# A third score buffer and two more projection buffers in a ViT tower's head loop, with the class key's columns copied by GpSimd one head later

## The reference

```python
def _layernorm(x, axis=-1, eps=1e-05): ...
for i in range(L):                                   # 4 layers
    qkv = h @ W_qkv[i]
    q, k, val = ...                                  # 16 heads of 64
    kr = (r @ W_r[i]).reshape(s_len, H, DH)
    AC = jnp.einsum('bqhd,bkhd->bhqk', q + u, k)
    BD = jnp.einsum('bqhd,khd->bhqk', q + v, kr)
    prob = jax.nn.softmax((AC + BD) * inv_sqrt_d, axis=-1)
    vec = jnp.einsum('bhqk,bkhd->bqhd', prob, val).reshape(b, s_len, H * DH)
    h = layer_norm(h + vec @ W_o[i], ln1_g[i], ln1_b[i])
    ff = jax.nn.relu(h @ W_ff1[i] + b_ff1[i]) @ W_ff2[i] + b_ff2[i]
    h = layer_norm(ff, ln2_g[i], ln2_b[i])
```

## Time and profile before

| | |
|---|---|
| median of three runs | 2712.31 us |
| the profiled execution | 2716.57 us |
| its span | 2714.8 us |
| granted TensorE clock, mean | 0.96 |
| TensorE busy | 2218.4 us, 82% |
| VectorE busy | 1825.3 us, 67% |
| ScalarE busy | 1611.2 us, 59% |
| GpSimd busy | 1180.7 us, 43% |

### The profile page before, as it was taken

One profiled execution on the slowest core, in us unless ns is written; L12 is line 12 of the kernel. 1 busy time (PEld: TensorE's weight loads), 2 busy tenths in 40 slices (PEclk: granted clock), 3 DMA queues, 4 the chain that ended last, 5 costly groups with the idle time before them and its releaser, 6 DMA issues. The chain is left out here.

```text
span 2714.8 us, 61320 instructions
## 1 busy us (share of the span) xinstructions
PE 2218.4 (82%) x19212; PEld 1637.8 (60%) x19213; DVE 1825.3 (67%) x5486; ACT 1611.2 (59%) x5053; POOL 1180.7 (43%) x2186
## 2 busy tenths in 40 slices
PE   0169989899988989889889889898898898733995
PEld 0146666666666666666666666676666666521663
DVE  8747777777767777777777777776777777643333
ACT  2136666666666667666666666666666666611221
POOL 3025445554555555544555555445645555102002
PEclk9679999999999999999999999999999999966998
DMA  5444333345553333454543333455433333074002
GB/s 168 95 109 104 92 92 92 92 107 138 137 141 93 92 92 92 108 135 114 148 105 89 94 92 92 126 128 152 105 91 93 92 93 92 18 190 140 29 27 78
DMA packets 386301, 282.99 MB, mean 104 GB/s; under 512 B 44859, under 2 KB 360371, under 8 KB 385355
## 3 DMA queue, kind: packets, MB, share of 16 engines
q1 hardware_dynamic: 379531, 262.37, 37.5%
q10 hardware_dynamic: 4864, 12.68, 1.3%
q0 software_dynamic: 1600, 4.23, 0.5%
HBM read 120.30 MB, written 57.82 MB: 66 GB/s over the span
## 5 line engine op out<-in xcount | busy, mean ns | idle before, releaser
L1248 ACT ACTIVATE E<-E,nb 128x257 f32<-128x257 f32 x1024 | 513.5, 510 | 38.3 <-DVE nb L1424 38.1
L969 PE MATMUL bk<-hin,w_sb 128*128 128x257 f16 x3072 | 424.7, 275 | 18.4 <-ACT rel L1186 9.0
L1424 DVE CUSTOM_DVE_ANT_0 E<-bk,cb 128x257 f32<-128x257 f32 x1024 | 390.1, 419 | 66.7 <-PE bk L1062 65.1
L1386 DVE TENSOR_TENSOR pt<-bk,pt 128x512 f16<-128x512 f32 x512 | 354.3, 692 | 63.7 <-ACT pt L1235 53.9
L1017 PE MATMUL bk<-ident,E 128*128 128x128 f32 x2048 | 323.2, 280 | 84.6 <-ACT E L1248 61.3
L969 PEld LDWEIGHTS bk<-hin,w_sb 128*128 128x128 f16 x3072 | 296.3, 98 | 72.5 <-issue 14.1
L1017 PEld LDWEIGHTS bk<-ident,E 128*128 128x128 f32 x2048 | 221.8, 141 | 164.1 <-ACT E L1248 150.5
L1235 ACT ACTIVATE pt<-bk 128x512 f16<-128x512 f32 x512 | 306.9, 599 | 6.5 <-PE bk L1017 6.5
L917 POOL TENSOR_SCALAR wf<-wf 128x256 f32<-128x256 f32 x216 | 92.8, 429 | 432.6 <-DMA wf<-in_w_dram 260.9
L1061 PE MATMUL bk<-kh,qs 128*128 128x257 f16 x1024 | 254.9, 275 | 9.7 <-DMA kl<-rk 9.5
L1062 PE MATMUL bk<-kl,qs 128*128 128x257 f16 x1024 | 254.5, 275 | 0.0
(11 more groups left out here) (275 smaller groups left out, 4406.3 us busy)
## 6 DMA issues: line engine op xcount, KB each, us to landing
qs<-rq SPq DMA_DIRECT2D x256, 128.5 KB, 3.5
kh<-rk SPq DMA_DIRECT2D x256, 128.5 KB, 3.2
kl<-rk SPq DMA_DIRECT2D x256, 128.5 KB, 3.6
wf<-in_w_dram SPq DMA_DIRECT2D x168, 128.0 KB, 2.6
w_split_dram<-wh SPq DMA_DIRECT2D x168, 128.0 KB, 2.2
w_sb<-w_split_dram SPq DMA_DIRECT2D x18, 1024.0 KB, 7.2
wf<-in_we_dram SPq DMA_DIRECT2D x96, 128.0 KB, 2.4
we_split_dram<-wh SPq DMA_DIRECT2D x96, 128.0 KB, 1.8
```

The source lines that it names most:

```text
L969: r = mm(bank[4 + s % 2][:, 0:S], wcol(a, C_QKV, k, 3 * HD, chunk_at(s)), hin[:, m, k, :], start=i == 0, stop=i == 5)
L1248: act.activation(E[:, h % 2, qt, :], E[:, h % 2, qt, :], ACT.Exp, bias=nb[:, 2 * h + qt:2 * h + qt + 1], scale=-1.0, accum_out=sums[:, qt, ...
L1386: v.tensor_tensor(pt[:, h, 1, :, 0:IMG], bank[2 + h % 2][:, :].rearrange("p (k s) -> p k s", k=QT), pt[:, h, 0, :, 0:IMG], ALU.subtract).t ...
L1424: v.tensor_tensor_reduce(E[:, h % 2, qt, :], bank[qt][:, 0:S], cb[:, h, :], -SCORE, 3e38, ALU.add, ALU.min, nb[:, 2 * h + qt:2 * h + qt + ...
```

## The change

`E` gets a third buffer (`EB` = 3) and `rel` four (`RB_` = 4), and all indices and waits follow: scores of head h wait for head h-3, `take_q` and `take_k` of slot s wait for the split of slot s-4. The class column's copy goes from ScalarE to GpSimd (`class_column`), where the one of head h-1 stands behind the split of slot h and ahead of the layer norm's step; the last one stands behind the loop. The memory for dynamic transfers' descriptors is 8192 bytes per partition; it was the default, twice that.

```diff
+EB, RB_ = 3, 4
...
-        E = sb("E", [P, 2, QT, S])
+        E = sb("E", [P, EB, QT, S])
...
-        rel = sb("rel", [P, 2, S])
+        rel = sb("rel", [P, RB_, S])
...
+            def class_column(at, h):
+
+                pool.wait_ge(e_ok, at(32, 2 * h + 2))
+                pool.tensor_copy(ecol[:, :, class_row(h, 0):class_row(h, 3):4], E[:, h % EB, :, CLS:S].broadcast_to([P, QT, 3])).then_inc(ecol_ok, 1)
...
                     for s in slots(h, kind):
                         split_projection(at1, s)
+                    if h:
+                        class_column(at, h - 1)
                     if h == 3 and kind.ln2:
                         ln2_newton(at)
...
                         ln2_lo(at, (B if kind.entry else b) - 1)
+                class_column(at, H - 1)
...
-                if s or not isinstance(at.g, int) or at.g:
-                    act.wait_ge(proj_lo, at(16, s - 1))
+                if at.g or s >= RB_:
+                    act.wait_ge(proj_lo, at(16, s + 1 - RB_))
...
-                    act.wait_ge(e_ok, at(32, 2 * h + 2))
-                    act.activation(ecol[:, :, class_row(h, 0):class_row(h, 3):4], E[:, h % 2, :, CLS:S].broadcast_to([P, QT, 3]), ACT.Copy).then_inc(ecol_ok, 1)
...
-                v.wait_ge(proj_lo, at(16, s - 1))
+                v.wait_ge(proj_lo, at(16, s + 1 - RB_))
...
-                    if h >= 2:
-                        v.wait_ge(t_done, at(16, h - 1))
-                        v.wait_ge(ecol_ok, at(16, h - 1))
+                    if h >= EB:
+                        v.wait_ge(t_done, at(16, h - EB + 1))
+                        v.wait_ge(ecol_ok, at(16, h - EB + 1))
...
-    nc = bacc.Bacc("TRN2", target_bir_lowering=False, num_devices=1)
+    nc = bacc.Bacc("TRN2", target_bir_lowering=False, num_devices=1, dynamic_dma_scratch_size=8192)
```

More of the change, by code:

```diff
@@ L860, in split_projection @@
                 pool.wait_ge(q_ok if j < NP else k_ok, n)
-                pool.tensor_scalar(dst[:, 0, j % NP, :], rel[:, s % 2, :], 1.0, 1.0, ALU.mult, ALU.mult).then_inc(proj_hi, 1)
+                pool.tensor_scalar(dst[:, 0, j % NP, :], rel[:, s % RB_, :], 1.0, 1.0, ALU.mult, ALU.mult).then_inc(proj_hi, 1)
                 pool.wait_ge(proj_hi, at(16, s + 1))
-                pool.tensor_tensor(dst[:, 1, j % NP, :], rel[:, s % 2, :], dst[:, 0, j % NP, :], ALU.subtract).then_inc(proj_lo, 1)
+                pool.tensor_tensor(dst[:, 1, j % NP, :], rel[:, s % RB_, :], dst[:, 0, j % NP, :], ALU.subtract).then_inc(proj_lo, 1)
             def ln2_newton(at):
@@ L930, in _ @@
                 pool.wait_ge(q_ok, c + 1)
-                pool.tensor_scalar(rq[:, 0, c, :], rel[:, 0, :], 1.0, 1.0, ALU.mult, ALU.mult).then_inc(proj_hi, 2)
+                pool.tensor_scalar(rq[:, 0, c, :], rel[:, s % RB_, :], 1.0, 1.0, ALU.mult, ALU.mult).then_inc(proj_hi, 2)
                 pool.wait_ge(proj_hi, s + 2)
-                pool.tensor_tensor(rq[:, 1, c, :], rel[:, 0, :], rq[:, 0, c, :], ALU.subtract).then_inc(proj_lo, 2)
+                pool.tensor_tensor(rq[:, 1, c, :], rel[:, s % RB_, :], rq[:, 0, c, :], ALU.subtract).then_inc(proj_lo, 2)
             def body(at, l, b, kind):
@@ L1017, in transposes @@
                         r = pe.transpose(bank[2 + h % 2][:, (kt * QT + qt) * P:(kt * QT + qt + 1) * P],
-                                         E[:, h % 2, qt, kt * P:(kt + 1) * P], ident[:, :])
+                                         E[:, h % EB, qt, kt * P:(kt + 1) * P], ident[:, :])
                 r.then_inc(t_done, 1)
@@ L1182, in take_q @@
                 act.wait_ge(proj_done, at(16, s + 1))
-                if s or not isinstance(at.g, int) or at.g:
-                    act.wait_ge(proj_lo, at(16, s - 1))
+                if at.g or s >= RB_:
+                    act.wait_ge(proj_lo, at(16, s + 1 - RB_))
                 j = chunk_at(s)
-                act.activation(rel[:, s % 2, :], bank[4 + s % 2][:, 0:S], ACT.Identity, bias=u16[:, j:j + 1]).then_inc(q_ok, 1)
+                act.activation(rel[:, s % RB_, :], bank[4 + s % 2][:, 0:S], ACT.Identity, bias=u16[:, j:j + 1]).then_inc(q_ok, 1)
             def v_part(at, u):
@@ L1247, in body @@
                         act.wait_ge(s_ok, at(32, 2 * h + qt + 1))
-                        act.activation(E[:, h % 2, qt, :], E[:, h % 2, qt, :], ACT.Exp, bias=nb[:, 2 * h + qt:2 * h + qt + 1],
+                        act.activation(E[:, h % EB, qt, :], E[:, h % EB, qt, :], ACT.Exp, bias=nb[:, 2 * h + qt:2 * h + qt + 1],
                                        scale=-1.0, accum_out=sums[:, qt, h:h + 1]).then_inc(e_ok, 1)
@@ L1324, in take_k @@
                 v.wait_ge(proj_done, at(16, s + 1))
-                v.wait_ge(proj_lo, at(16, s - 1))
-                v.tensor_tensor(rel[:, s % 2, :], bank[4 + s % 2][:, 0:S], kr16[:, j - NP, :], ALU.add).then_inc(k_ok, 1)
+                v.wait_ge(proj_lo, at(16, s + 1 - RB_))
+                v.tensor_tensor(rel[:, s % RB_, :], bank[4 + s % 2][:, 0:S], kr16[:, j - NP, :], ALU.add).then_inc(k_ok, 1)
             def v_part(at, u):
@@ L1423, in body @@
                         v.wait_ge(s_done, s_count)
-                        v.tensor_tensor_reduce(E[:, h % 2, qt, :], bank[qt][:, 0:S], cb[:, h, :], -SCORE, 3e38,
+                        v.tensor_tensor_reduce(E[:, h % EB, qt, :], bank[qt][:, 0:S], cb[:, h, :], -SCORE, 3e38,
                                                ALU.add, ALU.min, nb[:, 2 * h + qt:2 * h + qt + 1]).then_inc(s_ok, 1)
```

## The result

The changed kernel takes 2770.64 us (median of four runs, 2766.01 to 2773.58) against 2712.64 (median of four, 2710.78 to 2718.27): 1.0209 times the time of before, 95% interval 1.0187 to 1.0230. It is 58 us slower; forecast were 75, with 2787 us.

What follows compares the result with a forecast made beforehand. Heads run at ScalarE's pace, but GpSimd, without pause from split 2 to split 6, is the latest engine there. Median 2712.3 + 69 for late scores over all images + 5 for TensorE's clock = 2787 us; range 2740 to 2850.

Steps and rivals of the forecast that it cites:

- ScalarE sets the pace and its copy gives back 0.095 us a head: Head loop: ScalarE never pauses; dropping 16 class copies gives back 1.5 us per image, 49 us in all.
- GpSimd runs without pause from split 2 on, and the scores of heads 6, 7 and 8 wait for its copies: Regular image, head loop: scores of heads 6, 7 and 8 come 1.3, 2.5 and 2.07 us later.
- A copy takes 0.20 us of GpSimd: Each of 512 class copies on GpSimd takes 0.20 us, as the similar hcls copy does; 102 us in all.
- the whole walk: One regular image followed to the class key's transposes with durations from the profile: 2.07 + 0.64 - 0.32 = +2.4 us.
- Head 12 loses 0.64 more, and 0.32 come back to the key: Regular image after head 8: head 12 a further 0.64 us later, then 0.32 regained up to the class key's transposes.
- Closing images +1.8 each, first +0.2, last -1.3: Images outside the 27 regular ones: three closing images +5.4 us together, the first +0.2, the last -1.3.
- Four projection buffers could give 23 us: Head loop: removing VectorE's wait for projection splits gives some 15 us in 27 images, about 2.5 per closing one.
- The scratch costs nothing: Expert stage's 34 indirect transfers: halving the descriptor memory costs zero, 34 us at most; as a rival, chance 0.03.
- Three more stretches at 1.2 GHz, 5 us: TensorE: new pauses before heads 7 and 8 and the key bring three more slow-clock stretches, 1.8 us per image, 5 us.
- The rival of a faster kernel: Scores don't wait for GpSimd's copy, both gains are kept: 2712 - 72 = 2640 us, decided at head 8; chance 0.08.
- a GpSimd copy beside VectorE's work may take longer: Head loop: GpSimd shares SBUF interfaces with VectorE, so copies beside two-input work may exceed 0.20 us, raising the sum.

Runs made afterwards that it cites:

- the fastest kernel: The changed kernel with the class column's copy on VectorE instead of GpSimd, written by a TENSOR_REDUCE instead of a COPY: 2670.27 us, ratio 0.9827 against the kernel before.

## Why the prediction was right

It forecast slower, by this mechanism, with a range that held the time. (Its terms add up to 2786, and 2787 stands there; nothing hangs on it.) Step by step:

- *ScalarE sets the pace and its copy gives back 0.095 us a head.* Right for a head, a little too much for an image. With four buffers and the copy first, the scores of heads 10 to 14 of the thirteenth image come 1.24, 1.34, 1.43, 1.53 and 1.63 us earlier than before, 0.10 more with each head. Up to the key transposes that kernel gains 1.4 us per regular image and the fastest one 1.75; less the 0.45 of the projection buffers this is 0.95 and 1.3 of the 1.5. The 0.3 us per ACTIVATE of the Trainium skill ("ScalarE: Activation LUTs", Rules for kernel authors), stated there for one with its bias as an operand, which this copy has not, would have given 4.8 us per image; the fastest kernel gains 1.75.
- *GpSimd runs without pause from split 2 on, and the scores of heads 6, 7 and 8 wait for its copies.* Right. Forecast were 1.3, 2.5 and 2.07 us later; relative to the image's start it is 1.2, 2.2 and 1.7. The waits for the copy were to be 1.7, 1.4 and 0.7 us, and are 1.40, 1.22 and 0.62. In the stretch from split 2 to split 7 GpSimd pauses once, for 0.16 us within Newton's step.
- *A copy takes 0.20 us of GpSimd.* This term was too large. The copy lasts 0.193, near the hcls copy of the earlier trace rows, but what follows it starts 0.15 to 0.18 later (1043.45 to 1043.60, 1046.06 to 1046.24). I had argued for ScalarE that only start to next start counts and then took for GpSimd the spacing that most hcls copies have; behind three of the 32, those followed by the split of a key, the next instruction starts 0.158 later in the kernel before already. Five copies at 0.155 instead of 0.20 are 0.2 of the 0.3 us by which head 8 was overrated. Twelve stand in the whole walk: with 0.155 it gives 1.85 us per regular image instead of 2.4, and 1.7 were measured, so this is the term that was mis-sized.
- *Head 12 loses 0.64 more, and 0.32 come back to the key.* Measured: 0.52 and 0.53, with the same copies in both legs. Sum per regular image 1.7 instead of 2.4, 45.5 instead of 64.8 us in 27. This is where the forecast's 75 and the measured 58 part.
- *Closing images +1.8 each, first +0.2, last -1.3.* Measured 2.1, 0.3 and -1.5.
- *Four projection buffers could give 23 us.* Too much: 13 to 16 were measured, 0.45 per regular image and 1.7 per closing one instead of 0.6 and 2.5. VectorE's scores of head 8 come 0.92 us earlier, and half of that is lost again by head 10.
- *The scratch costs nothing.* Right.
- *Three more stretches at 1.2 GHz, 5 us.* The number came out by luck (6.4 us more outside the head loops, eight such stretches in the images of the profiled run instead of three), the reason did not. I had tied them to new pauses of TensorE of 1.4 and 1.0 us; in the thirteenth image of the changed kernel the longest in the head loop are 0.93 and 0.76, where before they were 0.82 and 0.64. The kernel with every copy twice has longer pauses (1.17 and 0.88) and shows only four stretches, and the fastest kernel, with none over 0.60, shows seven. The kernel before shows three, and with nothing but the scratch halved four, most of them in other images. Their number differs from profile to profile, and what sets it stays open.

The rival of a faster kernel asked whether GpSimd would be through copy 5 in time. It had asked for 1026.9, in the times of the earlier trace rows; copy 5 ended at 1029.1, 2.2 us too late. With the copy ahead of the split it ended at 1027.9: enough to take the loss away, still not enough for that rival's gain.

## What to carry to other kernels

An engine's idle share says nothing on whether it is early where a new wait meets it: follow its timeline through the stretch in which it has the most to do. If a buffer is released by an engine with other duties, the release belongs ahead of those duties on its queue; here the order of two neighbours was worth some 59 us, at no cost in memory, and a fourth buffer in its place 73. And when a small operation is moved to lighten an engine, try each engine that has slack, and more than one form of the instruction.

## What the runs showed of the hardware that was not expected

A COPY of six float32 values per partition on VectorE, from one SBUF buffer to another, waits for a GpSimd instruction that is under way: 255 of 512 took 0.17 to 0.77 us and ended 0.03 us after it. Of the other 257 those that began within a GpSimd instruction either started together with it or with at most 0.10 us of it left. A TENSOR_REDUCE that writes the same values took 0.141 to 0.165 us each time, beside the same GpSimd work. The Trainium skill ("SBUF — State Buffer", Who interferes with whom) describes an exclusive lock on a port pair that VectorE's instructions in a two-port mode share with GpSimd, held by the one that starts first for its whole instruction; the trace agrees, with the 255 copies that began second and ended 0.03 us after GpSimd. That this COPY is in such a mode no row says. What the prediction drew on, that a GpSimd copy beside VectorE's work may take longer, did not show: the 512 copies on GpSimd have a mean of 0.193 us and take at most 0.203. It was hardly tried, though: the VectorE instructions beside the hcls copies, `E<-bk,cb` and `rel<-bk,kr`, take one of their two inputs from PSUM (`bk`). What a copy takes beside an instruction with both inputs in SBUF no run shows, and the prediction's row of 0.203 did not show it either.

On GpSimd such a small copy holds up the next instruction for 0.13 to 0.18 us, depending on what follows (0.156 before a split, 0.128 before another copy); doubling all 512 left their mean at 0.193.
